# Moving the first code visit of TensorE's expert code into the gating stage, adding a fourth, and aligning TensorE's program

## The chip, the cores and the metric

The kernel runs on one core of one Trainium2 chip. Its time is the device time of one execution in microseconds (us); the median of three runs is 1102.18 us (1101.59 to 1102.27). TensorE (PE) does the matmuls, VectorE (DVE), ScalarE (ACT) and GpSimd (POOL) the rest, and SyncE (SP) issues most transfers.

## The reference, cut to what matters

The input x has 2 x 1024 tokens of 512 values. A mixture of experts, a mixer and the same mixture again are applied, each to the layernorm of x and added to x:

```python
x = x + 0.5 * ffn(layernorm(x))      # 8 experts, top 1, hidden 2048
x = x + attn(layernorm(x))           # projections, gates, cumsum, conv
x = x + 0.5 * ffn(layernorm(x))

# ffn
logits = tokens @ gate_weight.T
top1 = argmax(logits)
ranks = cumsum(one_hot(top1)) - 1            # place of a token in its expert
mask  = one_hot(top1) * (ranks < C)          # C = 320
dispatch = the tokens of each expert, gathered
hmid = gelu(dispatch @ wi[e])                # 512 -> 2048
eout = hmid @ wo[e]                          # 2048 -> 512
out  = probability of top1 * eout, back at the token's row
```

How many tokens an expert gets depends on the data, from a few to 320.

## The kernel before, in words

The program has three stages: layer 0 (gating, then eight experts), the mixer, layer 1 (gating, then eight experts). All products are split in a high and a low fp32r part, so each is three matmuls (L1212 to L1214 for `wi`, L1219 to L1221 for `wo`).

**Widths.** An expert's matmuls stream only as many columns as it has tokens, rounded up to one of six widths: 240, 256, 272, 288, 304, 320. The width is known only at run time, so TensorE's program holds the expert's code six times for each layer, once for each width (`run_240_0` to `run_320_0`, and `..._1`). DVE packs the eight width numbers in one integer (`pack_counts`, `code`), TensorE loads it in a register (L1471), and a chain of compares (`dispatch`, L1466, L1468) branches to the copy for the expert at hand. The copy ends in a branch back to the loop's head.

**Blocks of code.** The kernel lays out TensorE's program in blocks of `BLOCK` = 256 instructions. `addr_align(BLOCK, offset, max_nops=0)` puts the next instruction at slot `offset` of a block; the gap is filled with instructions that are never executed, and where one is needed a branch leads over it. The loop over the experts is aligned so (L1473), and each copy that has a visit starts at slot 0 of a block and ends with a lone branch in slot 255 (L1497, L1498).

**Visits.** `peek()` makes TensorE's instruction queue branch to that lone branch of the next copy (L1352), and it comes straight back (L1497, L1498). No matmul is run there. Each call also writes a hint for the next visit's branch (L1356): `marks` keeps the place where the call before stood, and the hint instruction stands at that place. `VISITED` = (3, 6) says that layer 0 visits the copies 240, 256 and 272, and layer 1 all six. In layer 0 all calls follow each other behind the gating's last matmuls (L1340); in layer 1 the first ones are spread over the end of the mixer. The copies without a visit (288, 304, 320 in layer 0) follow each other without gaps, so only the first of them starts at a block's start.

**The stage around the change.** In layer 0's gating TensorE goes through eight pairs of token tiles: `turn(p)` transposes them (L1267), `logits(p)` multiplies with the gate's weights (L1284), `folds(p)` adds four parts (L1296). `earlier()` (L1318, L1321) and `ranks()` (L1306, L1308) count the tokens before each one, `take_counts()` (L1326) counts all, and `tabulate` (L1340) builds a table of source rows. Then DVE makes indices of it, POOL gathers the rows of the first expert with three indirect DMAs (L475), ACT normalizes them to `dn` (L625), and TensorE, which waits at the loop's head (L1478), transposes `dn` (L1384) and begins the first expert. Meanwhile SP loads the first weights: 4 MB of x and 4 MB of weights in the first 25 us.

Of the kernel before, what the change touches and what calls it, by code (L numbers as in the profile page):

```python
# [43 lines left out]
BATCHES = 2  # L44
SPLIT = (8, 12)
HALF_B = (12, 14)
VISITED = (3, 6)
MOST = 12
PAIR = 2
PAIRED = TILES // PAIR  # L50
# [10 lines left out]
HALF = 256  # L61
STEPS = INTER // HALF
BLOCK = 256
WARM = 6
WARM_X1 = 14
ICS = HALF // P
# [8 lines left out]
def tiles_of(n, b):  # L75

    return slice(0, SPLIT[n]) if b == 0 else slice(SPLIT[n], TILES)
# [5 lines left out]
def build_kernel(nc, x, wuT, wvT, wg1T, wg2T, small_in, wi, wo, out):  # L83
# [6 lines left out]
    with ExitStack() as ctx:  # L90
# [1117 lines left out]
        def _(pe):  # L1208
# [25 lines left out]
            width = pe.alloc_register("width")  # L1234
            visits = [[], []]
            marks = []
            pe.wait_ge(pool_const, 3)
            def warm(times):

                for _ in range(times):  # L1240
                    pe.matmul(psT[1][:, :], ones[:, :], ones[:, :].unsqueeze(1).to_broadcast([P, DC, P]),
                              start=True, stop=True)

            warm(WARM)
            pe.wait_ge(pool_const, 8)
# [5 lines left out]
            for n, s in enumerate(layers):  # L1251
# [4 lines left out]
                def turn(p, s=s):  # L1256

                    for t in range(PAIR * p, PAIR * p + PAIR):
                        if s is layers[1]:
                            pe.wait_ge(d_addu, t + 1)  # L1260
                        elif t < GROUP:
                            pe.wait_ge(x_tile[t], 16)
                        else:
                            pe.wait_ge(x_in[p - GROUP // PAIR], 16)
                        to = turn_bank(s.xT_copied, t + 1)
                        for c in range(DC):
                            ins = pe.transpose(to[:, c * P:(c + 1) * P], xt[:, t, c * P:(c + 1) * P], ident[:, :])  # L1267
                        ins.then_inc(s.xT_done, 1)

                def logits(p, s=s):  # L1270

                    pe.wait_ge(s.xT_copied, PAIR * p + PAIR)
                    if p == 0:
                        if s is layers[0]:
                            pe.wait_ge(gates_set, 1)
                            pe.wait_ge(banks_set, 1)
                        else:
                            pe.wait_ge(d_vg, DC * GROUPS)
                    if p >= 2:
                        pe.wait_ge(s.lgT_copied, p - 1)  # L1280
                    first = PAIR * p % RING_T
                    for c in range(DC):
                        strip = slice(c * STRIP, (c + 1) * STRIP)
                        ins = pe.matmul(ps_logitT[p % 2][strip, :], gates[:, c, :],  # L1284
                                        xTt[:, first:first + PAIR, c * P:(c + 1) * P],
                                        start=True, stop=True, tile_position=(0, c * STRIP))
                    ins.then_inc(s.logits_done, 1)

                def folds(p, s=s, n=n):
                    pe.wait_ge(s.lgT_copied, p + 1)  # L1290
                    if p == 0 and s is layers[0]:
                        pe.wait_ge(fold_set, 1)
                    b = int(PAIR * p >= SPLIT[n])
                    first = PAIR * p - tiles_of(n, b).start
                    for j in range(PAIR):
                        ins = pe.matmul(ps_logit[b][:, first + j, :], lgT[:, p % 2, j * P:(j + 1) * P], fold[:, :],  # L1296
                                        start=True, stop=True)
                    ins.then_inc(s.folded, 1)
# [13 lines left out]
                def earlier(s=s, n=n):  # L1312

                    m = TILES - SPLIT[n]
                    pe.wait_ge(s.oh_done, 1)
                    pe.wait_ge(s.lgT_copied, PAIRED)
                    for t in range(SPLIT[n]):
                        pe.matmul(ps_rank[1][:, 0:m, :], ones[:, :], ohb[:, t, :].unsqueeze(1).to_broadcast([P, m, E]),  # L1318
                                  start=(t == 0), stop=False)
                    for t in range(SPLIT[n]):  # L1320
                        pe.matmul(ps_taken, ones[:, :], ohb[:, t, :], start=(t == 0), stop=False)  # L1321
# [24 lines left out]
                def peek(n=n):  # L1346

                    done = visits[n]
                    if done:
                        w = WIDTHS[len(done) - 1]  # L1350
                        done[-1] = nc.cur_bb
                        pe.br(f"visit_{w}_{n}").branch_hint(marks.pop())  # L1352
                        nc.switch_bb(f"visited_{w}_{n}", parent=done[-1])
                    if len(done) < VISITED[n]:
                        done.append(None)
                        marks.append(pe.mark_branch_hint_location())  # L1356

                if n == 0:
                    for p in range(PAIRED):
                        turn(p)  # L1360
                        if p == PAIRED - 1:
                            ranks(0)
                        if p >= 1:
                            logits(p - 1)
                        if p >= 2:
                            folds(p - 2)
                    logits(PAIRED - 1)
                    folds(PAIRED - 2)
                    folds(PAIRED - 1)
                earlier()  # L1370
                if n == 1:
                    tabulate(0, LT)
# [1 line left out]
                take_counts()  # L1374
                tabulate(LT * n, SPLIT[n])
                tabulate(SPLIT[n], TILES)
                for _ in range(3 + (n == 0)):
                    peek()

                def turn_tokens(e, c, s=s):  # L1380
# [57 lines left out]
                def turn_last(s=s):  # L1438

                    pe.wait_ge(s.out_dve, 3 * E)  # L1440
                    for c in range(DC):
                        pe.wait_ge(s.eoT_done, DC * E + c + 1)
                        for k, bank in HELD:
                            q, m = k * P, ROWS[k]
                            ins = pe.transpose(bank[0:m, c * P:(c + 1) * P], eoT[:, c, q:q + m], ident[:, :])
                            if c == DC - 1:
                                ins.then_inc(s.last_T, 1)
# [24 lines left out]
                pe.wait_ge(s.wi_lo, 1)  # L1472
                pe.addr_align(BLOCK, offset=BLOCK - 2, max_nops=0)  # L1473
                with pe.Fori(0, E) as e:
# [11 lines left out]
                turn_last()  # L1486
                pe.addr_align(BLOCK, offset=BLOCK - 1, max_nops=0)
                pe.br(f"done_{n}")
                over_bb = nc.cur_bb
                for k, w in enumerate(WIDTHS):  # L1490
                    with nc.body(f"run_{w}_{n}", parent=head, valid_engines=[pe.engine]):
                        expert(e, w)
                        pe.br(f"join_{n}")
                    if k >= VISITED[n]:
                        continue
                    with nc.body(f"visit_{w}_{n}", parent=visits[n][k], valid_engines=[pe.engine]):
                        pe.addr_align(BLOCK, offset=BLOCK - 1, max_nops=0)  # L1497
                        pe.br(f"visited_{w}_{n}")  # L1498
# [171 lines left out]
```

## Time and profile before

| | |
|---|---|
| profiled execution's own time | 1102.27 us |
| its span | 1100.5 us |
| PE busy | 1050.6 us (95%) |
| share of PE in the chain that ended last | 93% |
| DVE, ACT, POOL busy | 721.7, 544.2, 147.0 us |
| blocks of code fetched on queue q8 | 28, 0.46 MB |
| mean granted clock of TensorE | 0.973 |

An engine's busy time is the sum of its instructions, and matmuls overlap, so 95% is not 95% of TensorE's peak. [...] The chain follows the last instruction back to what released it, step by step; "issue" in it is time that no instruction in the profile explains.

### The profile page before, as it was taken

How to read it: one execution, taken by the hardware profiler on the slowest of the kernel's cores; microseconds unless marked ns; L12 is line 12 of the kernel's file. 1: busy time of each engine (PE TensorE's matmuls, PEld its weight loads, DVE VectorE, ACT ScalarE, POOL GpSimd, SP SyncE). 2: the span in 40 equal slices, each digit the busy share in tenths (PEclk: the TensorE clock that was granted, in tenths of full speed). 3: DMA queues.
4: the chain of work that ended last, by engine and by line, in shares of the span. 5: the costliest groups of instructions: out<-in, count | busy, mean ns of one | idle time of the engine just before them, and what ended most of it. 6: DMA issues, size and time to landing. Idle time of an engine off the chain costs nothing.

```text
span 1100.5 us, 20918 instructions
## 1 busy us (share of the span) xinstructions
PE 1050.6 (95%) x7912; PEld 994.7 (90%) x7912; DVE 721.7 (66%) x1089; ACT 544.2 (49%) x851; POOL 147.0 (13%) x135
## 2 busy tenths in 40 slices
PE   8699999999999999599999996999999999999995
PEld 6699999999999999478777776999999999999995
DVE  7566566766677777388685874557767677665652
ACT  4445454665556575253333234355656656554431
POOL 2201111113020210100000022002112021130101
PEclk9699999999999999899999996999999999999998
DMA  8458646566465651500011235346566564654410
GB/s 307 175 229 287 204 142 216 182 232 211 166 211 185 243 198 55 177 1 1 1 39 39 77 105 179 128 149 243 178 226 233 193 243 178 227 212 143 170 38 24
DMA packets 83277, 177.33 MB, mean 161 GB/s; under 512 B 4192, under 2 KB 4704, under 8 KB 83168
## 3 DMA queue, kind: packets, MB, share of 16 engines
q1 hardware_dynamic: 75488, 152.61, 39.5%
q0 software_dynamic: 7168, 23.07, 5.9%
q10 hardware_dynamic: 576, 1.05, 0.3%
q8 instruction: 28, 0.46, 0.2%
q14 instruction: 17, 0.14, 0.0%
HBM read 162.04 MB, written 18.87 MB: 164 GB/s over the span
## 4 chain that ended last, share of the span: by engine, by line
PE 93%; ACT 1%; DMA 1%; DVE 1%; issue 1%; POOL 1%; POOLq 0%; SPq 0%; ACTq 0%; DVEq 0%
PE psH L1213 13%; PE psH L1212 13%; PE psH L1214 13%; PE acc L1220 12%; PE acc L1221 12%; PE acc L1219 12%; PE acc L1212 3%; PE acc L1214 3%; PE acc L1213 3%; PE psT L1428 1%; PE psT L1267 1%; PE psH L1340 1%; PE acc L1384 1%; PE psH L1384 1%; PE psT L1533 1%
## 5 line engine op out<-in xcount | busy, mean ns | idle before, releaser
L1212 PE MATMUL psH<-dth,wih 128*128 128x240 f32 (+5 forms) x1024 | 294.2, 287 | 0.0
L1213 PE MATMUL psH<-dtl,wih 128*128 128x240 f32 (+5 forms) x1024 | 293.3, 286 | 0.0
L1220 PE MATMUL acc<-htl,woh 128*128 128x240 f32 (+5 forms) x1024 | 293.3, 286 | 0.0
L1221 PE MATMUL acc<-hth,wol 128*128 128x240 f32 (+5 forms) x1024 | 293.1, 286 | 0.0
L1214 PE MATMUL psH<-dth,wil 128*128 128x240 f32 (+5 forms) x1024 | 293.0, 286 | 0.0
L1219 PE MATMUL acc<-hth,woh 128*128 128x240 f32 (+5 forms) x1024 | 293.0, 286 | 0.0
L786 DVE TENSOR_TENSOR wol<-raw_wo,woh 128x1024 fp32r<-128x1024 f32 x128 | 155.7, 1223 | 146.3 <-ACT woh L608 146.3
L642 ACT ACTIVATE gel<-psH 128x320 f32<-128x320 f32 x256 | 112.0, 437 | 188.3 <-PE psH L1214 183.0
L608 ACT ACTIVATE woh<-raw_wo 128x1024 fp32r<-128x1024 f32 x128 | 134.3, 1057 | 132.2 <-PE acc L1221 132.2
L1212 PEld LDWEIGHTS psH<-dth,wih 128*128 128x128 f32 x1024 | 193.5, 189 | 0.4
L1213 PEld LDWEIGHTS psH<-dtl,wih 128*128 128x128 f32 x1024 | 193.5, 189 | 0.0
L1220 PEld LDWEIGHTS acc<-htl,woh 128*128 128x128 f32 x1024 | 193.5, 189 | 0.0
L1214 PEld LDWEIGHTS psH<-dth,wil 128*128 128x128 f32 x1024 | 193.5, 189 | 0.0
L1221 PEld LDWEIGHTS acc<-hth,wol 128*128 128x128 f32 x1024 | 193.5, 189 | 0.0
L1219 PEld LDWEIGHTS acc<-hth,woh 128*128 128x128 f32 x1024 | 193.5, 189 | 0.0
L786 DVE TENSOR_TENSOR wil<-raw_wi,wih 128x1024 fp32r<-128x1024 f32 x128 | 156.0, 1219 | 0.1
L597 ACT ACTIVATE wih<-raw_wi 128x1024 fp32r<-128x1024 f32 x128 | 134.6, 1053 | 0.0
L1022 DVE CAST hth<-gel 128x640 fp32r<-128x640 f32 x128 | 63.7, 498 | 94.5 <-ACT gel L642 94.0
L786 DVE TENSOR_TENSOR htl<-gel,hth 128x640 fp32r<-128x640 f32 x128 | 105.7, 826 | 4.4
L512 POOL DMA_INDIRECT out_x<-rows,dst_now x24 | 34.3, 1429 | 326.8 <-DVE rows L1067 322.5
L512 POOL DMA_INDIRECT x<-rows,dst_now x24 | 35.1, 1463 | 319.0 <-DVE rows L1067 314.8
L625 ACT ACTIVATE dn<-rows,facts_now 128x512 f32<-128x512 f32 x48 | 37.4, 808 | 47.2 <-DVE facts_now L1002 28.2
(194 smaller groups left out, 1163.8 us busy)
## 6 DMA issues: line engine op xcount, KB each, us to landing
raw_wi<-in_wi SPq DMA_DIRECT2D x64, 1024.0 KB, 5.1
raw_wo<-in_wo SPq DMA_DIRECT2D x64, 1024.0 KB, 5.3
out_x<-xt SPq DMA_DIRECT2D x4, 1024.0 KB, 5.8
xt<-in_x SPq DMA_DIRECT2D x6, 512.0 KB, 7.8
xt<-x SPq DMA_DIRECT2D x3, 1024.0 KB, 9.7
raw_u<-in_wuT SPq DMA_DIRECT2D x1, 1024.0 KB, 10.9
raw_u<-in_wvT SPq DMA_DIRECT2D x1, 1024.0 KB, 12.6
xt<-in_x ACTq DMA_DIRECT2D x2, 256.0 KB, 3.4
```

Of the source, the lines that this page charges most:

```text
L512: pool.indirect_dma_start(target[:, :], bass.IndirectOffsetOnAxis(ap=dst_now[0:m, a, k:k + 1], axis=0), rows[a][0:m, k, :], None).then_inc ...
L597: act.activation(wih[:, step % 2, :, :], raw_wi[k][:, :, (step % 2) * HALF:(step % 2 + 1) * HALF], copy).then_inc(s.wi_hi, 1)
L608: act.activation(woh[:, step % 2, :, :], raw_wo[k][:, (step % 2) * ICS:(step % 2 + 1) * ICS, :], copy).then_inc(s.wo_hi, 1)
L642: act.activation(gel[:, step % 2, j, :], psH[j][:, 0:CAP], ACT.Gelu).then_inc(s.gelu_done, 1)
L786: return dve.tensor_tensor(out, full, hi.bitcast(F32), ALU.subtract)
L1022: dve.tensor_copy(hth[:, k, :, :], gel[:, k, :, :]).then_inc(s.ht_hi, 1)
L1212: pe.matmul(out, lh, rh, start=first, stop=False)
L1213: pe.matmul(out, lh, rl, start=False, stop=False)
L1214: return pe.matmul(out, ll, rh, start=False, stop=last)
L1219: pe.matmul(out, lh, rh, start=False, stop=False, skip_group_check=True)
L1220: pe.matmul(out, lh, rl, start=False, stop=False, skip_group_check=True)
L1221: return pe.matmul(out, ll, rh, start=False, stop=False, skip_group_check=True)
```

## The change

Four edits, all in TensorE's program. `VISITED[0]` goes from 3 to 4, so the copy 288 of layer 0 gets a visit too and is padded to a full block, which moves the copies 304 and 320 and all code behind them by 34 slots. A call of `peek()` is put into the gating of layer 0 behind `folds(2)`, in the round p = 4; it writes no branch, it only marks the place of the first hint. A second is put behind the last `folds`; it branches to the copy 240. Three calls are left behind the gating, which branch to 256, 272 and 288. And the whole of TensorE's program is aligned at its start so that a block ends 153 slots behind its first matmul.

```diff
-VISITED = (3, 6)
+VISITED = (4, 6)
+TO_HINT = 153
...
             marks = []
+            pe.addr_align(BLOCK, offset=BLOCK - TO_HINT, max_nops=0)
             pe.wait_ge(pool_const, 3)
...
                         if p >= 2:
                             folds(p - 2)
+                        if p == 4:
+                            peek()
                     logits(PAIRED - 1)
                     folds(PAIRED - 2)
                     folds(PAIRED - 1)
+                    peek()
                 earlier()
...
-                for _ in range(3 + (n == 0)):
+                for _ in range(3):
                     peek()
```

Lines behind the edits carry higher numbers in the kernel after: L1352 is L1354, L1356 is L1358, L1318 is L1320, L1340 is L1342.

TensorE's program before, at the end of layer 0's gating, from the last round's products to the loop over the experts (psH and acc are PSUM banks, ohb the chosen expert of each token, at_facts and at_lane what the table is made of):

```order
L1296 MATMUL acc<-fold,lgT 128x8 x4
L1318 MATMUL psH<-ohb,ones 128x64 x8
L1321 MATMUL acc<-ohb,ones 128x8 x8
L1306 MATMUL psH<-ohb,tri 128x64
...
L1340 MATMUL psH<-at_facts,at_lane 128x96 x16
L1356 BRANCH_PREFETCH_HINT
L1352 UNCONDITIONAL_BRANCH
L1356 BRANCH_PREFETCH_HINT
L1352 UNCONDITIONAL_BRANCH
L1356 BRANCH_PREFETCH_HINT
L1352 UNCONDITIONAL_BRANCH
L1471 TENSOR_LOAD code
```

The three visits and their hints stand together between the table's matmuls and the load of the code, each hint directly ahead of its own branch. The same place in the kernel after:

```order
L1298 MATMUL acc<-fold,lgT 128x8 x4
L1354 UNCONDITIONAL_BRANCH
L1358 BRANCH_PREFETCH_HINT
L1320 MATMUL psH<-ohb,ones 128x64 x8
L1323 MATMUL acc<-ohb,ones 128x8 x8
...
L1342 MATMUL psH<-at_facts,at_lane 128x96 x16
L1354 UNCONDITIONAL_BRANCH
L1358 BRANCH_PREFETCH_HINT
L1354 UNCONDITIONAL_BRANCH
L1358 BRANCH_PREFETCH_HINT
L1354 UNCONDITIONAL_BRANCH
L1476 TENSOR_LOAD code
```

One branch and one hint have moved ahead of `earlier()`; three branches are still behind the table. The third place is the middle of the gating in the kernel after, where the first hint now stands:

```order
L1269 MATMUL psT<-ident,xt 128x128 x8
L1286 MATMUL acc<-xTt,gates 32x256 x4
L1298 MATMUL acc<-fold,lgT 128x8 x2
L1358 BRANCH_PREFETCH_HINT
L1269 MATMUL psT<-ident,xt 128x128 x8
```

The hint for the copy 240 stands three rounds and the tail of the gating ahead of its branch, where there was nothing before.

## Rows read from the trace of the kernel before

**Rows 1.** Waits of TensorE: for whom, us in total, times, longest.
```profile
PE acc L1384 <- ACT dn L625: 18.3, 2, 9.3
...
PE psT L1241 <- POOL ones L431: 1.3, 1, 1.3
```

**Rows 2.** Chain that ended last, 22 to 49 us (start us, us, what).
```profile
26.35 0.24 DVE ohb L850
...
26.63 0.20 PE psH L1306
...
27.19 6.93 PE psH L1340 x32
...
41.81 0.82 ACT dn L625
42.63 0.74 issue
43.38 1.54 PE acc L1384 x6
```

**Rows 3.** The same chain, 660 to 684 us, layer 1.
```profile
676.51 0.82 ACT dn L625
677.33 0.14 issue
```

**Rows 4.** Visit branches (L1352) one by one: ns min/median/max, start; layer 0, then layer 1.
```profile
L1352 PEldq COMPARE_BRANCH  x1: 3308/3308/3308, 31.5 to 31.5; - x1
...
L1352 PEldq COMPARE_BRANCH  x1: 2420/2420/2420, 35.4 to 35.4; - x1
...
L1352 PEldq COMPARE_BRANCH  x1: 2935/2935/2935, 38.4 to 38.4; - x1
...
L1352 PEldq COMPARE_BRANCH  x1: 417/417/417, 646.2 to 646.2; - x1
...
L1352 PEldq COMPARE_BRANCH  x1: 334/334/334, 665.8 to 665.8; - x1
...
L1352 PEldq COMPARE_BRANCH  x1: 3446/3446/3446, 667.0 to 667.0; - x1
...
L1352 PEldq COMPARE_BRANCH  x1: 2513/2513/2513, 671.2 to 671.2; - x1
```

**Rows 5.** TensorE's queue at the loop's entry: layer 0, layer 1; then the waiting instruction.
```profile
L1474 PEldq FUSED_REGOPS  x1: 53/53/53, 42.9 to 42.9; - x1
...
L1474 PEldq FUSED_REGOPS  x1: 56/56/56, 675.0 to 675.0; - x1
...
L1478 PEldq FUSED_REGOPS  x1: 53/53/53, 43.3 to 43.3; - x1
```

**Rows 6.** TensorE's queue, 20 to 26 us: first wait of earlier().
```profile
L1316 PEldq EVENT_SEMAPHORE  x1: 51/51/51, 23.9 to 23.9; - x1
```

**Rows 7.** TensorE in order of time, 23 to 30 us (start us, us; idle before).
```profile
24.34 0.39 PE L1318 MATMUL psH<-ohb,ones 128*128 128x64 bf16 x8
24.57 0.35 PE L1321 MATMUL acc<-ohb,ones 128*128 128x8 bf16 x8
26.63 0.20 PE L1306 MATMUL psH<-ohb,tri 128*128 128x64 bf16 x1 [1.72 <-DVE ohb L850]
```

**Rows 8.** DMA queues in 12 to 19 us, then 19 to 20 us: packets, MB, share.
```profile
q1 hardware_dynamic: 1371, 2.71, 104.7%
...
q8 instruction: 1, 0.02, 6.9%
```

**Rows 9.** Compares of the expert dispatch, 60 to 448 us.
```profile
L1466 PEldq COMPARE_BRANCH  x17: 64/76/211, 99.7 to 398.4; - x17
```

**Rows 10.** Stretches: length, busy of PE, PEld, DVE, ACT, POOL; PEclk, DMA share, GB/s.
```profile
27.00:28.00 1.00, 1.00 (x14) 1.00 (x10) 0.97 (x6) 0.98 (x2) 0.00 (x0) 0.67 0.00 0
...
47.00:48.00 1.00, 1.00 (x11) 0.94 (x10) 0.55 (x2) 1.00 (x2) 0.00 (x0) 0.59 0.81 283
...
682.00:683.00 1.00, 1.00 (x9) 0.89 (x7) 1.00 (x2) 0.65 (x1) 0.00 (x0) 0.65 0.77 184
```

## The prediction

> **What bounds the kernel now.** I read the page first: PE is busy for 95% of the span and holds 93% of the chain that ended last, so only what delays a matmul costs time. Then the waits of TensorE: almost all of its idle time is in three waits, of which two are for `dn` in the first expert of each layer, 18.3 us together [rows 1]. In these two gaps the visits are made. So the change is about one gap, 34 to 43 us of layer 0, and the question is what ends it.
>
> The chain through that gap goes from the table's last matmul (34.1 us) over DVE, POOL and the gather to ACT, whose third `dn` runs from 41.81 for 0.82 us, to 42.63. Then stand 0.74 us of "issue", and only at 43.38 TensorE's first transposition [rows 2]. At the same place of layer 1 the issue time is 0.14 us [rows 3]. So in layer 0 TensorE comes about 0.60 us later than its data allows. Its instruction queue shows why: the three visit branches take 3308, 2420 and 2935 ns from 31.5 us on [rows 4]; behind them come the load of the code and the loop's entry, and the queue is at L1474 only at 42.9 us, when `dn` is already 0.3 us old; the waiting instruction L1478 follows at 43.3 [rows 5], some 0.3 us later, which I take for the step into the loop's own block. In layer 1 the queue is at L1474 at 675.0, 2.3 us ahead of its `dn` (677.33) [rows 3, 5]. There the visits do not set the end of the gap, in layer 0 they do.
>
> **The change, part by part.**
>
> *Three visits behind the table in place of three, of which the first is prepared.* In layer 0 a visit of the copy 240 moves out of the gap and one of 288 comes in. What the three in the gap will cost is read from layer 1, whose last three visits stand in a row behind the table too: 334, 3446 and 2513 ns from 665.8 us, and the loop's entry at 675.0 [rows 4, 5]. That is 9.2 us from first branch to entry, against 42.9 - 31.5 = 11.4 us in layer 0 now. The first is cheap because the visit before it has already brought its neighbour (the visit of 256 in layer 0 took 0.9 us less than that of 240). So the queue should be at the entry at 31.5 + 9.2 = 40.7, with the step into the loop's block at 41.0, 1.6 us ahead of `dn`. TensorE then starts 0.60 us earlier: **-0.60 us**. This gain is capped, however early the queue arrives, since the gather and ACT end the wait next.
>
> *What the 0.60 us are worth.* [...] I take 0.45. [...]
>
> *The visit of 240 ahead of earlier().* Its branch will be reached about where the queue now meets L1316, at 23.9 us [rows 6]. It is beside DVE's work: TensorE idles for 1.72 us until DVE's `ohb` is ready, and starts L1306 at 26.63 [rows 2, 7]. Behind the visit stand L1318 and L1321, which need 24.92 - 24.34 = 0.58 us [rows 7], and the way back from a visit takes about 0.5 us (34.8 to 35.3: 31.5 + 3.31, then the two returns and the hint, by the start of the next visit at 35.4). So the branch may end as late as 26.63 - 0.58 - 0.5 = **25.5 us** at no cost. If its code is there it ends at 24.3 (417 ns, the first visit of layer 1, whose hint stands 4 us ahead [rows 4]). Cost 0, cover 1.2 us.
>
> *Will its code be there?* This is the price that the trace does not show. The hint now runs in the round p = 4, about 15.7 us. From 12 to 19 us the data engines are full (104.7%), and in these 7 us no block of code is fetched; the one fetch of the stage falls in 19 to 20 us [rows 8]. [...] Upper bound: the hint is lost, and the branch fetches for itself: 23.9 + 3.3 (the first visit of layer 0, without data beside it) + up to 1 for the last data = 27.2 to 28.2, which costs 1.7 to 2.7 us. [...]
>
> *The visit of 288.* Now that copy is fetched by the expert loop's first branch; the first expert uses it (its matmuls have 288 columns), beside matmuls in TensorE's queue, so 0 is gained. In layer 0 the other copies were not fetched again: 17 compares from 60 to 448 us take 211 ns at most [rows 9]. [...]
>
> *Alignment at the start and 34 slots of shift.* The added branch at the start is done before 1.3 us, while TensorE waits for `ones` [rows 1]: 0. The blocks' borders in the mixer move, where TensorE has matmuls queued and the visits of 0.4 to 1.5 us are already hidden: 0. The last three visits of layer 1 keep their order, and 2.3 us of slack.
>
> **Sum.** 0.60 us earlier, worth 0.45; nothing else on the path. Made against the profiled execution, 1102.27 us (span 1100.5 and 1.8 around it): 1101.8. Against the median of 1102.18, which is 0.09 lower: **1101.7 us**. A difference under 0.2%, 2.2 us, could not be told from no change here, so this is a forecast of no measurable change.
>
> **The rivals.**
>
> *Late code (slower side).* The branch to 240 at 23.9 us ends behind 25.5, and the queue stands while `ohb` is ready. Each us later delays L1306, the table (6.93 us [rows 2]), the gather and the first expert by a us. [...] Against: 8 us between hint and branch. [...] With the hint lost: 1.7 to 2.7 less 0.45, so 1103.4 to 1104.4. It decides from 25.9 us on; it would pass 0.2% only from 28.2 on.
>
> *The head stays late.* If the first visit behind the table is not prepared (256 not brought by the visit of 240, or already gone), the gap holds three full visits again, 3.3 + 2.4 + 2.9 us, and the queue arrives at 42.9 as now: 1102.2. For: nothing in layer 0 shows a block that outlives 7 us of other fetches. Against: layer 1's 334 ns, for a visit that likewise stands behind the table while the one before it stands in the mixer [rows 4]; and the 211 ns [rows 9]. [...]
>
> *A start that misses.* If the aligned start lies in a block that is not loaded, TensorE's first matmul comes 3.3 us later, at 4.6 us in place of 1.3, and the gating, in which PE is busy without a gap, is 2 to 3 us late: about 1104.5. Against: the kernel now steps into the next block in this stage with no fetch ahead of it.
>
> *The clock.* The half clock begins in 27 to 28 us (0.67 in that slice [rows 10]). If other timing keeps it full through the table's 6.93 us, half of that goes, 3.5 us: 1098.2. Nothing in the change adds work there.
>
> **How the numbers follow.** Forecast 63%; late code 20%, of which a third with the full price; the head stays late 10%; a start that misses 3%; the clock 4%. The forecast's own range is 1101.2 to 1102.3: worth 0.30 or 0.60, and the spread of three runs, 0.68 us. For 8 in 10 it must reach into late code above, and below to a rise of the clock that comes a little earlier: 1100.5 to 1103.5. Faster by over 0.2% (under 1100.0) comes from the clock alone, 5%; slower (over 1104.4) from half of the missed start and the end of late code, 5%; the rest, 90%, is within 0.2%.
>
> **What would show it right or wrong.** Issue time ahead of the first L1384 (L1389 in the kernel after) of 0.1 to 0.2 us in place of 0.74; the entry of the loop by 41 us; visit branches of about 0.4, 0.3, 3.4 and 2.5 us in layer 0, the first at 23.9; the table's matmuls starting at 27.2 as now. A first visit of over 1.6 us, or L1306 behind 26.7, makes late code true; a gap in the gating before 5 us the missed start; three long visits behind the table the head that stays late. A change of over 1 us in either direction with the table and the first `dn` in place would mean that I missed where the time lies.

## The result, and the profile after

The kernel after takes 1110.25 us (median of five runs, 1107.79 to 1110.61), the kernel before beside it 1101.60 (1101.40 to 1102.27): the ratio is 1.0072 with a 95% interval of 1.0057 to 1.0087. The change makes the kernel slower by 8 us, where 1101.7 and no measurable difference were forecast. The profiled execution of the kernel after took 1108.56 us, its span is 1106.8, 6.3 us longer than that of before; what follows accounts for these 6.3. That the timed median lies 1.7 us above this execution is not explained by it. One execution of e3_early_only, described below, took 4362.95 us and is left out of its ratio and of the median given for it.

The waits of TensorE (for whom; us in total, times, longest) have two new large entries that no engine and no data cause, both called issue (a third, on L1538, is 0.3 us):

```profile
PE acc L1389 <- ACT dn L626: 18.3, 2, 9.3
PE psT L1243 <- DMA xt<-x: 10.0, 1, 10.0
PE psH L1320 <- issue: 6.1, 2, 5.5
PE acc L1395 <- issue: 2.6, 1, 2.6
```

Against [rows 1] the wait for `dn` is the same, and 8.7 us of issue have come, while the 1.72 us for `ohb` [rows 7] are gone: they now lie inside the first of the new waits. That one is in the gating. The chain that ended last, 23 to 47 us (start us, us, what):

```profile
23.09 0.36 PE psH L1320 x7
23.46 5.46 issue
28.92 0.21 PE psH L1320
...
29.82 6.14 PE psH L1342 x32
...
43.77 0.82 ACT dn L626
44.59 0.67 issue
45.26 1.54 PE acc L1389 x6
```

TensorE does 7 of the 8 matmuls of earlier()'s first loop, then stands for 5.46 us, and does the eighth. A break in the middle of a loop without a wait is not data. By a count of the records it is the border between two blocks, the place where the program crosses from one block of code to the next: a matmul leaves one record on PE and one on PEld, one of plain fp32 two on each (L1342: 16 in the program, 32 in the trace), and from the first matmul to the break stand 410 records of matmuls, weight loads and TensorE's queue, two of them in the copy that was visited, against 153 + 256 = 409 slots. e9 below moves this border by 13 slots, and the break moves with it by six matmuls (398 records, 140 + 256 = 396 slots). So the table starts at 29.82 in place of 27.19 [rows 2], though this execution had `ohb` ready 2 us earlier than before (24.58 against 26.59). Of these 2.6 us, 1.9 reach the first expert, since the table itself takes 6.14 us in place of 6.93: the granted clock is 0.56 in 34 to 35 us and 1.00 in 35 to 36, where it was 0.50 to the table's end before. The last lines answer to the end of [rows 2]: the 0.74 us of issue that the change was to remove are still 0.67. The visit branches (L1354) in layer 0, ns and start, one view per stretch (PEldq marks what TensorE's instruction queue does: branches, waits, register instructions):

```profile
L1354 PEldq COMPARE_BRANCH  x1: 328/328/328, 21.8 to 21.8; - x1
...
L1354 PEldq COMPARE_BRANCH  x1: 318/318/318, 33.8 to 33.8; - x1
...
L1354 PEldq COMPARE_BRANCH  x1: 4396/4396/4396, 34.9 to 34.9; - x1
...
L1354 PEldq COMPARE_BRANCH  x1: 3413/3413/3413, 40.0 to 40.0; - x1
```

The early visit finds its code, and so does the next. The stall is not a visit's. The DMA queues, 12 to 24 us and then 24 to 26 us (packets, MB, share) say what it waits for:

```profile
q1 hardware_dynamic: 2325, 4.60, 104.0%
q8 instruction: 1, 0.02, 0.6%
...
q8 instruction: 2, 0.03, 11.7%
```

The second new wait is in the expert loop. The compares of the third expert's dispatch, and the branch that leaves the loop:

```profile
L1471 PEldq COMPARE_BRANCH  x3: 69/76/3665, 156.9 to 157.2; - x3
...
L1493 PEldq COMPARE_BRANCH  x1: 3417/3417/3417, 452.4 to 452.4; - x1
```

[Rows 9] had 211 ns as the longest of these. TensorE has 1.2 us of work queued behind the first, to 158.37, and then runs dry; what that does to the clock is in the stretches after it (length, busy of PE, PEld, DVE, ACT, POOL, granted clock, DMA share, GB/s):

```profile
160.93 0.25 PE L1395 MATMUL acc<-ones 128*128 128x2 bf16 x4 [2.56 <-issue]
```
```profile
160.00:161.00 1.00, 0.07 (x3) 0.07 (x4) 0.00 (x0) 0.00 (x0) 0.00 (x0) 1.00 0.00 0
161.00:162.00 1.00, 1.00 (x9) 0.93 (x10) 0.00 (x0) 0.00 (x0) 0.00 (x0) 0.58 0.06 16
...
163.00:164.00 1.00, 1.00 (x6) 1.00 (x6) 1.00 (x2) 0.00 (x0) 0.41 (x1) 0.50 0.00 0
164.00:165.00 1.00, 1.00 (x8) 1.00 (x7) 1.00 (x2) 0.26 (x1) 1.00 (x1) 0.71 0.00 0
165.00:166.00 1.00, 1.00 (x10) 1.00 (x9) 0.21 (x1) 0.18 (x1) 1.00 (x1) 1.00 0.00 0
```

After a gap of 2.56 us the granted clock is 0.50 of full for some 3 us, from 161.2 to 164.6. Cut at fixed events, one profiled execution of each kernel gives this table (us; the columns are defined below it, and the experiments are in the next section):

```
run              table  1st token  exp 2-3  exp 3-4  layer 0  between  layer 1   span
before            27.0       43.4     55.8     51.6    402.9    231.2    423.0  1100.5
after             29.6       45.3     58.4     52.6    406.0    231.0    424.5  1106.8
e1_align_only     26.1       43.5     55.8     51.1    402.7    230.7    422.6  1099.5
e2_fourth_only    27.3       47.4     55.8     51.1    402.3    232.3    424.3  1106.3
e3_early_only     29.2       45.0     58.4     52.6    406.9    230.9    423.4  1106.2
e4_no_align       29.9       44.4     58.2     52.6    406.0    231.5    424.2  1106.1
e5_hint_kept      25.1       41.3     55.8     51.1    402.4    230.0    424.1  1097.8
e6_early_nohint   28.7       43.3     55.9     51.0    401.8    230.4    425.4  1100.9
e7_skip_256       26.8       45.0     58.1     52.6    411.1    230.4    425.2  1111.7
e8_hint56         29.1       44.2     55.8     51.1    402.2    231.9    423.4  1101.8
e9_hint140        30.0       44.3     58.2     52.5    405.5    233.6    425.0  1108.4
e10_hint130       29.0       44.7     55.9     51.0    402.6    231.9    424.8  1104.0
e11_after_nohint  28.6       43.9     55.8     51.1    402.5    230.7    423.4  1100.5
e12_kept_plain    26.8       44.5     55.8     51.0    403.1    234.0    422.8  1104.4
```

"Table" is the start of the table's weights, "1st token" that of the first transposition of an expert; "exp 2-3" and "exp 3-4" run from clear_acc() of the second and third expert to that of the next; "layer 0" from the first token to turn_last(), "between" on to layer 1's first token, "layer 1" to the end. For after against before: 45.3 - 43.4 = +1.9 in the gating, 406.0 - 402.9 = +3.1 in layer 0's experts (2.6 in the second step, 1.0 in the third, the rest is rounding and other steps), -0.2 between, +1.5 in layer 1. The 3.4 us branch that leaves the loop costs nothing: the x load that ends that gap is awaited for 10.0 us beside it.

### The profile page after: what moved, and what is told of

Read it like the earlier page. It is cut to its first block, busy times and chain, and to the rows that moved or that the text cites. A ratio compares the mean times of both kernels' runs of the same rounds, so it can differ in the third digit from the quotient of the medians.

```text
span 1106.8 us, 20923 instructions
## 1 busy us (share of the span) xinstructions
PE 1047.5 (95%) x7912; PEld 990.7 (90%) x7912; DVE 721.2 (65%) x1089; ACT 544.1 (49%) x851; POOL 147.3 (13%) x135
## 3 DMA queue, kind: packets, MB, share of 16 engines
q10 hardware_dynamic: 576, 1.05, 0.3%
## 4 chain that ended last, share of the span: by engine, by line
PE 91%; issue 2%; DVE 2%; DMA 2%; ACT 1%; POOL 1%; POOLq 0%; SPq 0%; ACTq 0%; DVEq 0%
PE psH L1214 13%; PE psH L1213 13%; PE psH L1215 13%; PE acc L1221 11%; PE acc L1222 11%; PE acc L1220 11%; PE acc L1213 3%; PE acc L1215 3%; PE acc L1214 3%; PE psT L1269 1%; PE psT L1433 1%; PE acc L1389 1%; PE psH L1389 1%; PE acc L1286 1%; PE acc L1298 1%
```

## The experiments

Two things needed a cause: why a block was missing in earlier(), and why copies that before stayed for 400 us were fetched again. The first four kernels take the change apart.

**Alignment alone**

```
against the kernel before:
+TO_HINT = 153
+            pe.addr_align(BLOCK, offset=BLOCK - TO_HINT, max_nops=0)
```

> Only the alignment at TensorE's start; the visits stay as before (none early, three in the gap, of which the fourth copy is not one). Theory (the loss has two sources: the block of code behind the early visit, which is not fetched in time, and copies of the expert that are fetched again because a fourth one is visited): neither is here, so the time is that of before, 1101.6 within 0.5 us, all compares of the expert loop in layer 0 under 350 ns. Rival (the shift of the blocks' borders by itself is what costs): 1104 to 1110, with a gap of TensorE's queue in the gating or a branch of over 2 us in the expert loop.

1101.40 us, ratio 0.9993 (0.9979 to 1.0008). The 17 compares of the loop from 60 us on are as before:

```profile
L1468 PEldq COMPARE_BRANCH  x17: 64/76/211, 100.1 to 398.4; - x17
```

The compare that leads to the first expert is not: it takes 2295 ns at 44.7 us in place of 344, against the expectation. TensorE has work queued there, and its step to the second expert is as before within 0.2 us. So the shift of the start and of the blocks' borders is free when it is made alone, and the rival is out.

**The fourth visit alone**

```
against the kernel before:
-VISITED = (3, 6)
+VISITED = (4, 6)
-                for _ in range(3 + (n == 0)):
+                for _ in range(3 + 2 * (n == 0)):
```

> No early visit and no alignment; layer 0 visits four copies, all behind the table. A fourth full visit in the gap takes about 3 us, so by the gap alone the queue comes to the loop at 45.9 us in place of 42.9 and the time is 1101.6 + 3.0 = 1104.6. Theory (the fourth copy pushes others out): the expert loop shows branches of over 2 us besides (the second or third expert, the one that leaves the loop, the first of layer 1), worth 2.9 + 2 or so: 1108 to 1110. Rival (the copies are pushed out by the early visit or the alignment): the loop's branches stay at 211 ns or less and the time is 1104.6.

Ratio 1.0042 (1.0025 to 1.0058), 1107.17 us. My theory fell: the loop's compares stay short (L1467), no copy is lost. The time is 2.6 us above the rival's number too. The price is first the visit itself:

```profile
L1467 PEldq COMPARE_BRANCH  x17: 64/76/352, 103.7 to 401.8; - x17
```
```profile
42.06 0.82 ACT dn L626
42.88 4.50 issue
```

4.50 us of issue in place of 0.74, and the first token 4.0 us later. Layer 0's experts take 402.3 us, as before. "Between" has 1.1 and "layer 1" 1.3 more, of which more below.

**The early visit alone**

```
against the kernel after:
-VISITED = (4, 6)
+VISITED = (3, 6)
-                for _ in range(3):
+                for _ in range(3 - (n == 0)):
```

> The alignment and the early visit of 240 as changed, but three copies visited as before (two behind the table). Theory: the code behind the early visit stalls TensorE as in the changed kernel (queue gap of over 4 us that ends near 29, table's matmuls from 29.8, first transposition of the expert near 44.7 to 45.3), +1.3 to 1.9 us, and the expert loop is as before: 1102.9 to 1103.5. Rival (the early visit is also what makes the copies go): branches of over 2 us in the expert loop, 1106 to 1110.

Ratio 1.0045 (1.0030 to 1.0060), 1107.54 us. The rival holds: with only three copies visited the stall is there (3.54 us, to 28.52) and so is the branch of the third expert. It is the early visit, with its hint, that pushes a copy out:

```profile
L1471 PEldq COMPARE_BRANCH  x2: 69/1874/3680, 157.5 to 157.7; - x2
```

**The change without its alignment**

```
against the kernel after:
-            pe.addr_align(BLOCK, offset=BLOCK - TO_HINT, max_nops=0)
```

> The changed kernel without the alignment at the start: the hint then stands 8 slots behind a block's start, and the next border comes in the table instead of inside earlier(). Theory (the hint takes the place of the fetch of the next block, wherever the border is): the stall stays but moves to the table (its matmuls broken by 2 to 3 us or more), and the expert loop's long branches stay: 1108 to 1111. Rival (the place of the border, set by the alignment, makes the stall): table from 27.2 without a break, 1106 to 1108.5.

1110.31 us, ratio 1.0067 (1.0052 to 1.0083). The break leaves earlier(), as the theory had it, but it does not stand in the table: it comes two matmuls into take_counts() (L1327), just ahead of it. 0.7 us stay ahead of earlier(), and both long branches of the loop stay (3548 and 3514 ns):

```profile
27.11 0.05 PE acc L1327 x2
27.16 2.61 issue
29.77 0.30 PE acc L1327 x6
```

The next four vary the hint and the place of the visit.

**The hint early, the visit behind the table**

```
against the kernel before:
+            pe.addr_align(BLOCK, offset=BLOCK - TO_HINT, max_nops=0)
+                        if p == 4:
+                            peek()
-                for _ in range(3 + (n == 0)):
+                for _ in range(3):
```

> Alignment and three visits behind the table as before, but the hint of the copy 240 stays in the round p = 4, 15 us ahead of its visit. Theory (the hint takes the place of the fetch of the next block): no fetch of the next block until TensorE needs it inside earlier(), so the queue stands there for about 3 us with no visit beside it, and the table starts 1 to 2 us later than in the run with the alignment alone (26.1). Second theory (two fetches at once, which come when a visit finds its code ready and both it and the way back ask for the next block, leave less room for the copies): such a pair appears at the first visit behind the table, and the expert loop fetches copies again (third expert's branch over 2 us): 1105 to 1108. Rival to the second (only a visit that is made ahead of the table does it): loop as before, 1101.5 to 1103.

1100.08 us, ratio 0.9992 (0.9975 to 1.0010). The first theory fell as I had put it: no stall in earlier(). The next block was there on time, although the hint stands at the very same slot of the same block as in the change. And the visit 17 us later still finds its code:

```profile
L1354 PEldq COMPARE_BRANCH  x1: 423/423/423, 29.4 to 29.4; - x1
```

So the hint does not displace the next block whenever it is given. What differs is where the hinted branch stands: in the change in the block that is running, here in the next one. The second theory expected two fetches at once at the first visit; they come at the first expert instead (45.00 and 45.29 us), and the third expert is fine. In the next run a pair does stand at the first visit behind the table (33.95 and 34.66 us), again with no copy lost: the second theory is out too.

**The visit early, the hint directly ahead of it**

```
against the kernel before:
+            pe.addr_align(BLOCK, offset=BLOCK - TO_HINT, max_nops=0)
                     folds(PAIRED - 1)
+                    peek()
+                    peek()
-                for _ in range(3 + (n == 0)):
+                for _ in range(3 - (n == 0)):
```

> Alignment and the early visit of 240, its hint directly ahead of the branch, so that the branch fetches for itself; three copies visited. Theory: the next block is fetched on time, so earlier() is not broken, but the branch itself takes 3.3 us or more from 23.5 us and the table starts 1 to 2.5 us later than 26.1. The expert loop: if two fetches at once (from a prepared visit) are what makes copies go, no branch over 400 ns in the loop and 1102 to 1104; if any early visit does it (more code between the first copy and its use), the third expert's branch takes over 2 us as in the changed kernel and the time is 1106 to 1108.

1102.45 us, ratio 1.0003 (0.9987 to 1.0019); the visit takes 3404 ns, the table starts at 28.7, and no copy is lost:

```profile
L1470 PEldq COMPARE_BRANCH  x17: 64/76/349, 99.1 to 397.3; - x17
```

So an early visit alone loses no copy either. It takes the long hint and the early visit together.

**Only 240 and 272 visited**

```
against the kernel before (peek() and the visits' code go by LOOKED):
+LOOKED = ((240, 272), (240, 256, 272, 288, 304, 320))
-                for _ in range(3 + (n == 0)):
+                for _ in range(3):
+                        if n == 0 and w == 256:
+                            pe.addr_align(BLOCK, offset=BLOCK - 1, max_nops=0)
```

The copy 256 keeps its full block, so the layout is that of before.

> The kernel before, but layer 0 visits only the copies 240 and 272, both behind the table (each visit also brings the block behind it). Theory (a visit behind the table costs its 2.4 to 3.5 us in the gap, and a visit brings its neighbour): the queue is at the loop by about 40.3 instead of 42.9, the first transposition comes 0.1 to 0.2 us behind dn instead of 0.74, no branch over 400 ns in the expert loop, 1101.0 to 1101.5, at most 0.6 us faster. Rival (without its own visit the copy 256 or a neighbour is missing): a branch of over 2 us at the eighth expert or earlier, 1102 to 1105.

1112.64 us, ratio 1.0086 (1.0061 to 1.0111): 11 us more than expected, and over 7 more than the rival gave. The visit of 272 alone takes 4525 ns, and then the first and the third expert's branches take 5461 and 3448:

```profile
L1467 PEldq COMPARE_BRANCH  x3: 64/78/5461, 46.1 to 46.3; - x3
...
L1467 PEldq COMPARE_BRANCH  x1: 3448/3448/3448, 162.4 to 162.4; - x1
```

One visit fewer made the visits no shorter and lost two blocks. The layout is that of before; what differs is which visits are made, and with it the order in which the blocks come.

**The alignment at another offset**

```
against the kernel after:
-TO_HINT = 153
+TO_HINT = 56
```

> The changed kernel with its start aligned elsewhere (TO_HINT 56 instead of 153): the whole program up to the load of the code is 97 slots further on in its block, so a border comes early in the warm-up, the hint stands in the middle of a block and the next border comes between the hint and the early visit. Theory (the stall in earlier() comes from a border behind the early visit whose block was not fetched): no stall there, the table starts at 27.2 or earlier, and the copies fetched again in the expert loop remain: 1.9 us less than the changed kernel, 1107 to 1109. Rival (the border does not matter, the stall is the visit's own fetches behind the data): stall as before in this stage, 1110.

1102.81 us, ratio 1.0013 (0.9998 to 1.0028). One number gives back 7 of the 8 us. The table is hardly earlier (29.1, now behind a visit of 2927 ns), but layer 0's experts are back at 402.2. Both the theory (1107 to 1109, with copies fetched again) and the rival (1110) were wrong: what I had taken for two effects went together.

```
place            0  1  2  3  4  5  6  7
before, e1, e2   8  9  2  3  4  5  6  7
after, e3, e4    0  1  2  3  4  7  8  9      (4 came to 2, 2 over 4, 5 to 3, 3 over 5, then 4 over 6)
e5, e6, e8       9  1  2  3  4  6  7  8      (4 at 3, 5 at 4, then 3 over 4 and 4 over 5)
```

The rule was then put to the test before the runs: it says that 10 slots decide.

**TO_HINT 140: branch at slot 251 of the running block**

```
against the kernel after:
-TO_HINT = 153
+TO_HINT = 140
```

> The changed kernel with its start 13 slots further on in the block (TO_HINT 140 instead of 153): the early branch to 240 is then the slot 251 of 256 of its block, still the block in which its hint stands. Theory (a hint whose branch lies in the running block brings its target in place of the next block; every sequential block is put in the place behind the running one of eight, so a next block fetched late pushes out a copy): as in the changed kernel. The visit finds its code (about 330 ns), two fetches at once near 24.5, a stall in front of or in earlier() until 28 to 29, and in the expert loop a third expert's branch over 2 us and a leaving branch over 2 us: 1109 to 1111. Rival (the few slots between hint and border matter by time, not by the block in which the branch stands): something between this run and the next one, 1104 to 1107.

**TO_HINT 130: branch at slot 5 of the next block**

```
against the kernel after:
-TO_HINT = 153
+TO_HINT = 130
```

> The same 10 slots further (TO_HINT 130): the early branch to 240 is now slot 5 of the following block. Theory: the hint no longer takes the place of the next block, which is fetched by 18 us; the target 240 is asked for only at the border just ahead of the branch and waits for the data until 24.5, so the visit takes 3 us or more, but earlier() is not broken; 4@3, 5@4, then 3 again in place of 4, 6 and 7 behind: the third expert (272) and the end of the loop find their code, the branches of the fourth and eighth expert ask for one block each beside their work (325 to 350 ns). 1102 to 1103.5, 7 us less than the run before. Rival: as the changed kernel, 1108 to 1111.

1111.37 us, ratio 1.0081 (1.0067 to 1.0094), against 1104.68 us, ratio 1.0016 (1.0007 to 1.0025), on the same chip: 6.7 us for ten slots, and the intervals are far apart. Both times are about 1 us above their expected ranges, on a chip where the kernel before takes 1102.73. The two profiled executions differ by less, 1110.11 against 1105.73. In order of time, with idle time and its cause in brackets, 140 and then 130:

```profile
24.98 0.19 PE L1320 MATMUL psH<-ohb,ones 128*128 128x64 bf16 x1 [0.66 <-issue]
28.91 0.56 PE L1320 MATMUL psH<-ohb,ones 128*128 128x64 bf16 x7 [3.73 <-issue]
```
```profile
27.91 0.58 PE L1320 MATMUL psH<-ohb,ones 128*128 128x64 bf16 x8 [4.21 <-issue]
```

With 140 the border falls behind the first matmul, as counted, and breaks the loop there; with 130 the break is the visit itself. The branches: visit, third expert, end of the loop, for 140 and then 130:

```profile
L1354 PEldq COMPARE_BRANCH  x1: 334/334/334, 23.7 to 23.7; - x1
...
L1471 PEldq COMPARE_BRANCH  x2: 69/1718/3366, 156.0 to 156.1; - x2
...
L1493 PEldq COMPARE_BRANCH  x1: 3777/3777/3777, 450.8 to 450.8; - x1
```
```profile
L1354 PEldq COMPARE_BRANCH  x1: 3875/3875/3875, 23.1 to 23.1; - x1
...
L1471 PEldq COMPARE_BRANCH  x2: 69/138/207, 157.2 to 157.3; - x2
...
L1493 PEldq COMPARE_BRANCH  x1: 313/313/313, 448.4 to 448.4; - x1
```

Every one as the rule has it. With the early branch in the hint's own block (140) the visit is 3.5 us cheaper and the kernel 6.7 us slower. In the profiles the second step of the experts differs by 2.3 us and the third by 1.5: a missing copy costs its gap and then the half clock behind it, 3.8 us, about 3 of them in the layer's total (405.5 against 402.6). 1.7 more lie "between", which the rule says nothing of, and the 2.3 us between the difference of the medians (6.7) and that of the profiled executions (4.4) lie in no profile. So the rule is shown for the branches and for about 3 us of the 6.7.

**The change, hint directly ahead of the early branch**

```
against the kernel after:
-                        if p == 4:
-                            peek()
                     folds(PAIRED - 1)
+                    peek()
                     peek()
```

> The changed kernel with the hint of 240 moved from round p = 4 to directly ahead of its early branch; four copies visited, alignment as changed. Theory: no copy is pushed out before its use (no branch over 400 ns in the expert loop of layer 0), the visit fetches for itself (3.4 us, table from 28 to 29 less what the profile's phase gives), the fourth visit fits into the gap; some of the time of the second experiment's layer 1 (its mixer and gap, 1.1 us) is here too: 1102.5 to 1104.5. Rival (the fourth copy is what makes the loss once the visit is early): branches over 2 us in the loop, 1107 to 1111.

1104.14 us, ratio 1.0021 (1.0004 to 1.0037). With four copies, the early visit and the alignment all kept, 6 of the 8 us go when the hint moves:

```profile
L1470 PEldq COMPARE_BRANCH  x17: 64/76/350, 100.4 to 398.6; - x17
```

**The kernel before with the hint alone moved**

```
against the kernel before:
+                        if p == 4:
+                            peek()
-                for _ in range(3 + (n == 0)):
+                for _ in range(3):
```

> The kernel before with one edit: the hint of the copy 240 stands in round p = 4, its visit stays behind the table (no alignment, three visits). Theory (a hint whose branch lies in a later block takes nothing from the next block; its target is fetched at the border in front of that branch): the first visit behind the table takes about 0.4 us in place of 3.3, the queue is at the loop by 40 us in place of 42.9 and the first transposition follows dn within 0.2 us instead of 0.74, no branch over 400 ns in layer 0's expert loop: 0.3 to 0.6 us faster than before in its gap, 1101.0 beside 1101.6, which a comparison of this kind may just not resolve. Rival (the place that 3 takes from 4 in the ring of blocks costs later): a branch of over 2 us in the loop, 1103 to 1105.

1101.33 us, ratio 1.0002 (0.9991 to 1.0014): no gain. In its profiled execution (1106.12 us, the slowest of its twelve, so not typical) the first visit took 2337 ns and not 0.4: without the alignment the border before the table comes late, and by the rule the target is asked for only there (fetch at 30.98, branch at 31.01). The later visits and the first expert's branch (2722 ns at 45.7) slid with it, and 2.29 us of issue stand behind `dn`. In e5, whose border is earlier, the target is fetched at 24.54 and the issue time is 0.14. e5 has the lowest median of all (1100.08) but its interval holds 1; no version was found that is measurably faster than before.

## Why the prediction was wrong

**Three visits behind the table, entry of the loop at 41, -0.60 us: wrong.** The first was cheap as said (318 ns). The other two took 4396 and 3413 ns, not 3446 and 2513, since for the first of these the block 6 and the head's block 3 were fetched at once (35.38 and 35.50 us) and took 1.60 and 2.13 us, where the two fetches at 35.52 and 39.03 in before took 0.96 each. In the layer 1 rows that I had priced them by, such a pair lies 0.62 us apart (666.87 and 667.49), and in e9, where it is 0.71 us apart, this visit takes 3292 ns. The last visit scatters besides: 2428 ns in e10, 3328 in e8. One row was thin ground for either. They also began 2.3 us later, with the table. The entry came at 44.9, behind `dn` (44.59), and the issue time stayed, 0.67.

**The 0.60 us worth 0.45: not shown.** No run shows this term of the sum. The granted clock rose from 0.50 to 1.00 of full 3.3 us behind the first token in the kernel after (48.53 against 45.26), 4.4 in before (47.81) and 4.5 in e5 (45.76), where the first token came 2.1 us earlier than in before and the ratio is 0.9992; in the other kernels it was 3 to 5.7, and 12.4 in e7. With differences of this size no gain of half a microsecond can be read off.

**"Will its code be there?": right, but the wrong question.** The visit took 328 ns at 21.8 us. The hint ran at 12.55 us and not at 15.7; the fetch came 3.8 us behind it, at 16.31. I asked only for the block of 240. That the rival's upper price, 2.7 us, is near the shift of the table, 2.6, is luck: another block was late, for another reason, and 1.9 us of it reached the first expert.

**"In layer 0 the other copies were not fetched again", cost 0: wrong, and the largest term.** 3.1 us in the profile, 3.8 with the clock behind it by e9 against e10. The row was right ([rows 9]); what I took from it, that copies stay once they are in, was not. By the rule they stayed because in the kernel before every block had come in order, one place behind the other. Distance alone is not what makes a copy absent: the branch to the third expert's copy, three blocks away, takes 207 ns in before, e1, e2, e5, e6, e8 and e10 to e12, and 3366 to 3680 ns in after, e3, e4, e7 and e9.

**Alignment and 34 slots of shift, 0: half right.** For the start it is 0 (e1, 0.9993). But the offset decides in which block the branch stands, and with it all else (e9, e10): an edit that costs nothing alone was not free beside the hint. The 34 slots move layer 1's visits. All kernels with four copies (after, e2, e4, e8 to e11) show visits of 2.3 to 3.9 us in layer 1's mixer, where those with three copies had 0.3 to 2.5. Their "between" is 230.7 to 233.6 against 230.0 to 234.0 of the others, so no cost can be told; one of up to 1 us is not excluded.

**The visit of 288, 0: not shown.** Behind the table a fourth visit costs 4.0 us (e2). In the change the early visit made room for it: without it (e3) the first token is only 0.3 us earlier in the profile. But by the ratios the kernel with four copies is the slower one in both pairs that differ by it: 1.0072 against 1.0045 (after, e3) and 1.0021 against 1.0003 (e11, e6), 2 to 3 us. The intervals of each pair touch, so this is not settled; some of the 8 us may be the fourth copy's and the 34 slots'.

**Layer 1, not in the sum: +1.5 us in the profile.** In the kernel after the branch of layer 1's second expert takes 2439 ns (at 744.5), and over 2.3 us in e2, e4, e5, e6, e7, e9, e10 and e11 too; in before, e1, e3, e8 and e12 it is at most 357 ns. In all of the former the block behind the head was not fetched at the loop's entry, and in all of the latter it was, some us later than asked for (681.10 in before). The step from layer 1's first expert to the second is 60.3 to 61.5 us long in the former and 59.3 to 59.9 in the latter, so it costs about 1 us. What decides whether that fetch is made is not settled: the request seems to be lost when the first expert's branch comes before it is served, but no run varied this alone.

**Also open:** why e7 misses what it does, and the 1.7 us between the profiled execution and the median of the kernel after. Each profile is one execution, and medians of the kernel before differ by 1.3 us between the chips used.
